# Decay arguments in a Mamba mixer: from six-row matmuls to biased Relus on ScalarE, with the order of three queues changed

## The reference, cut to what matters

```
proj = hidden_states @ in_proj_w.T          # gate (z), x, B, C, dt
hBC  = silu(conv1d(x, B, C; 4 taps))        # B, C shared by 16 of 128 heads
dt   = softplus(dt + dt_bias);  A_dt = -exp(A_log) * dt
A_cumsum = cumsum(A_dt, inside each chunk of 128 tokens)
Lmat = exp(A_cumsum[l] - A_cumsum[s])  for l >= s, else 0
Y_diag = ((C_l . B_s) * Lmat) @ (x * dt)
states = (B * exp(A_cumsum[-1] - A_cumsum))^T @ (x * dt)      # each chunk
new_states: each chunk's state * exp(its last A_cumsum) + the next one's
Y_off  = (C @ carried state) * exp(A_cumsum)
y = rms_norm(Y_diag + Y_off + D * x) * norm_w * silu(gate)
out = y @ out_proj_w.T
```

## Time and profile before

| | |
|---|---|
| profiled execution | 2141.5 us, its span 2139.8 us |
| mean granted clock of TensorE | 0.997 of full |
| TensorE (PE) busy | 2102.7 us, 98% of the span |
| VectorE (DVE) busy | 1689.4 us, 79% |
| ScalarE (ACT) busy | 1401.8 us, 66% |
| GpSimd (POOL) busy | 881.4 us, 41% |
| DMA | 241.89 MB, mean 113 GB/s |
| table loads at the lines of silu and Exp (L1263, L1286) | 127 each, 1283 ns |
| argument matmuls (L1051) | 1024 |

### The profile page before, as it was taken

One profiled execution on the slowest core, in us unless ns is written; L12 is line 12 of the kernel. 1 busy time (PEld: TensorE's weight loads), 2 busy tenths in 40 slices (PEclk: granted clock), 3 DMA queues, 4 the chain that ended last, 5 costly groups with the idle time before them and its releaser, 6 DMA issues.

```text
span 2139.8 us, 37480 instructions
## 1 busy us (share of the span) xinstructions
PE 2102.7 (98%) x13386; PEld 1732.0 (81%) x13386; DVE 1689.4 (79%) x2679; ACT 1401.8 (66%) x1918; POOL 881.4 (41%) x622
## 2 busy tenths in 40 slices
PE   7999998999999999999999999999999999999999
PEld 6788876888888888888888888888888888878887
DVE  7555468988888888888898889898888888876554
ACT  5322277878787777777787877787777778752221
POOL 1222134545454545444454544544544545422221
PEclk9999998999999999999999999999999999999999
DMA  5543224233333333232333333342333233255441
GB/s 201 177 146 138 61 94 125 90 109 103 100 112 101 105 96 108 95 122 91 100 112 101 101 98 114 105 122 96 100 101 112 90 104 109 97 186 177 135 147 40
DMA packets 128644, 241.89 MB, mean 113 GB/s; under 512 B 14048, under 2 KB 48608, under 8 KB 128224
## 3 DMA queue, kind: packets, MB, share of 16 engines
q1 hardware_dynamic: 128480, 239.73, 34.9%
HBM read 234.17 MB, written 5.51 MB: 112 GB/s over the span
## 4 chain that ended last, share of the span: by engine, by line
PE 90%; DVE 3%; issue 3%; ACT 2%; DMA 1%; POOL 1%; SPq 0%; DVEq 0%; POOLq 0%; ACTq 0%
PE ring L1013 35%; PE ring L1113 16%; PE bank L412 6%; PE bank_e L412 6%; PE yt L1094 6%; PE st L1078 4%; PE yt L1100 4%; PE xt L1065 3%; PE bank_e L424 3%; PE bank L424 3%; PE arg L1051 2%; PE xt L1026 1%; PE bank L654 1%; DMA w_raw<-w_in 0%; DVE xr L304 0%
## 5 line engine op out<-in xcount | busy, mean ns | idle before, releaser
L1013 PE MATMUL ring<-m_lnt,w_sb 128*128 128x512 f32 x3456 | 859.9, 399 | 1.2 <-DVE xc L1440 1.2
L1013 PEld LDWEIGHTS ring<-m_lnt,w_sb 128*128 128x128 f32 x3456 | 633.0, 189 | 127.1 <-DVE xc L1440 1.5
L1673 POOL TENSOR_TENSOR w_sb<-w_raw,w_sb 128x512 fp32r<-128x512 f32 x288 | 401.7, 1400 | 177.3 <-ACT w_sb L1246 177.0
L1688 POOL TENSOR_TENSOR ysq<-ysq,y 128x512 f32<-128x512 f32 x126 | 162.8, 1292 | 652.8 <-ACT y L1290 652.8
L1113 PE MATMUL ring<-wo,ygs 128*128 128x512 f32 x1536 | 369.4, 390 | 2.0 <-issue 2.0
L1113 PEld LDWEIGHTS ring<-wo,ygs 128*128 128x128 f32 x1536 | 287.3, 188 | 63.2 <-issue 2.6
L1440 DVE SCALAR_TENSOR_TENSOR xc<-ring,cw,xc 128x511 f32<-128x511 f32 (+2 forms) x384 | 286.0, 745 | 23.0 <-ACT xc L1258 13.9
L1258 ACT ACTIVATE xc<-ring,cb,cw 128x512 f32<-128x512 f32 x128 | 99.2, 775 | 215.4 <-PE ring L1013 215.4
L1678 POOL TENSOR_TENSOR wo<-wo_raw,wo 128x512 fp32r<-128x512 f32 x128 | 214.0, 1672 | 0.0
L1246 ACT ACTIVATE w_sb<-w_raw 128x512 fp32r<-128x512 f32 x288 | 177.0, 619 | 26.8 <-DMA w_raw<-w_in 26.8
L1094 PE MATMUL yt<-em,x_dt 128*64 128x128 f32 x2048 | 183.7, 279 | 3.2 <-DVE state L1482 3.2
(11 more groups left out here) (203 smaller groups left out, 3159.2 us busy)
## 6 DMA issues: line engine op xcount, KB each, us to landing
w_raw<-w_in SPq DMA_DIRECT2D x288, 256.0 KB, 4.2
ce<-e_t SPq DMA_DIRECT2D x128, 384.0 KB, 4.1
wo_raw<-w_out SPq DMA_DIRECT2D x128, 256.0 KB, 4.4
f_gu_q<-gu_w SPq DMA_DIRECT2D x28, 512.0 KB, 3.7
f_gu_zr<-gu_z SPq DMA_DIRECT2D x28, 512.0 KB, 4.5
f_gu_sr<-gu_s SPq DMA_DIRECT2D x28, 512.0 KB, 5.3
f_dn_q<-dn_w SPq DMA_DIRECT2D x28, 256.0 KB, 3.5
f_dn_zr<-dn_z SPq DMA_DIRECT2D x28, 256.0 KB, 4.0
```

The source lines that it names most:

```text
L1013: mm = nc.tensor.matmul(dst[:], w_sb[:, u % WR, wp, k * P:(k + 1) * P], lnt[:, xp, k, b * S:(b + 1) * S], start=(i == 0), stop=(i == 3 * K ...
L1673: nc.gpsimd.tensor_tensor(w_sb[:, u % WR, 1], w_raw[:, u % NR], w_sb[:, u % WR, 0].bitcast(F32), ALU.subtract).then_inc(w_lo, 1)
```

## The change

- `arguments(k)`, the bf16 parts, `a_left`, `a_right` and what fills them go. The float32 sums go to memory (`c_t`), and SP broadcasts the two heads' rows to all partitions, into one of two buffers `cum_b`, two pairs ahead. The sums by token, `cum_q`, come out of one more matmul.
- `clamp(k)`: eight Relus over 128 columns on ScalarE, from and to `cum_b`, with scale -1 and the token's sum as bias. `exponent(k)` is then one Exp from `cum_b` into ARG.
- ScalarE: `clamp(k+1)` stands where `exponent(k)` stood. In odd steps `exponent(k+1)` follows it; in even steps it is the last thing of the step, behind the silus, `y_high`, `square`, and `activate_bc`.
- VectorE: `mask_em(k)` goes ahead of `scale_x(k)` and `gate(k-1)`.
- SP: in each step the next units' weights, then `load_out`, then the sums, then `ce`; `load_gu(0, 0)` of the last step comes behind them.
- The opening of the mixer: Exps of sums of later steps (`later`, `sum_later`) give the decay of the states in place of differences, products and transposes; `sum_chunks` gives each chunk's last Exp; `dt_q` is copied earlier.
- `ysq` has half the size, with `square_sums(0)` five steps earlier.

```diff
+                def clamp(k):
+                    act.wait_ge(c_loaded[k % 2], 16 * (k // 2 + 1))
+                    if k == 0:
+                        act.wait_ge(cumq_done, B)
+                    for h in range(2):
+                        for c in range(CPB):
+                            at = slice(c * CS, (c + 1) * CS)
+                            last = nc.scalar.activation(cum_b[:, k % 2, h, at], cum_b[:, k % 2, h, at], ACT.Relu, scale=-1.0,
+                                                        bias=cum_q[:, k, c, h:h + 1])
+                    last.then_inc(arg_clamped, 1)
+
                 def exponent(k):
-                    act.wait_ge(arg_mm, k + 1)
-                    part = ARG[:].rearrange("p h t -> p (h t)")
-                    nc.scalar.activation(part, part, ACT.Relu, scale=-1.0).then_inc(arg_clamped, 1)
                     act.wait_ge(arg_clamped, k + 1)
-                    nc.scalar.activation(part, part, ACT.Exp, scale=-1.0).then_inc(exp_done, 1)
+                    need(act, em_done, k)
+                    if k == 0:
+                        act.wait_ge(btok_done, 1)
+                        act.wait_ge(decq_done, B)
+                    nc.scalar.activation(ARG[:], cum_b[:, k % 2], ACT.Exp, scale=-1.0).then_inc(exp_done, 1)
...
-                    if k < K:
-                        exponent(k)
+                    if k + 1 < K:
+                        clamp(k + 1)
                     for g in gram_in(k):
                         copy_btok(g)
                     if k + 1 < K:
+                        if k % 2:
+                            exponent(k + 1)
                         activate_x(k + 1)
                         activate_z(k + 1)
...
                         tap(unit)
                         if unit[0] == "c":
                             activate_bc(unit[1])
+                    if k + 1 < K and k % 2 == 0:
+                        exponent(k + 1)
...
-                    if k < K:
-                        scale_x(k)
                     if k == 0:
                         conv(("x", 1))
+                        scale_x(0)
                         decay_c(0)
+                        mask_em(0)
+                    elif k < K:
+                        mask_em(k)
+                        scale_x(k)
                     if 1 <= k <= K:
                         gate(k - 1)
                     if k < K:
-                        mask_em(k)
...
                 for k in range(K):
                     if k > 0:
-                        load_units(k + 1)
-                    if k + 1 < K:
-                        load_args(k + 1)
-                    if k == K - 1:
-
-                        sp.wait_ge(prj_mm, NU)
-                        sp.wait_ge(conv_done, len(CONVED))
-                        tiles.load_gu(sp, 0, 0)
+                        load_units(units_of(k + 1))
                     if 1 <= k < K:
                         load_out(k - 1 if k < K - 1 else K - 1)
                     if k == K - 2:
                         load_out(K - 2)
+                    if k + 2 < K:
+                        load_args(k + 2)
+                    if k + 1 < K:
+                        load_decay(k + 1)
+                    if k == K - 1:
+
+                        sp.wait_ge(prj_mm, NU)
+                        sp.wait_ge(conv_done, len(CONVED))
+                        tiles.load_gu(sp, 0, 0)
```

More of the change, by code:

```diff
@@ L740, in build @@
         a_dt = sbp("a_dt", [P, B, CPB * H])
-        cum = sbp("cum", [P, T, CS])
-        diff = sbp("diff", [P, T, CS])
-        dec_h = sbp("dec_h", [P, B * S])
+        cum = sbp("cum", [P, B * S])
         e_cum = sbp("e_cum", [P, B * S])
-        rest = sbp("rest", [P, B * S])
-        parts = sbp("parts", [P, 3, B * S], BF16)
-        e_end = sbp("e_end", [P, T])
+        later = sbp("later", [P, P])
+        gap_p = sbp("gap_p", [P, 14 * P + 8])
         a_neg = sbp("a_neg", [P, H])
@@ L1339, in scalar @@
                 nc.scalar.activation(low[:], low[:], ACT.Ln, bias=1.0).then_inc(softplus, 1)
+                for b in range(B):
+                    act.wait_ge(adt_done, b + 1)
+                    nc.scalar.activation(dt_q[:, b * JP:(b + 1) * JP],
+                                         (XT, ST)[b][:].rearrange("p (c j h) -> p j c h", c=CPB, h=2), ACT.Copy)\
+                        .then_inc(dtq_done, 1)
                 w_high(("x", 1))
@@ L1342, in scalar @@
                 tap(("x", 0))
+                for b in range(B):
+                    act.wait_ge(cum_mm, b + 1)
+                    nc.scalar.activation(cum[:, b * S:(b + 1) * S], ARG[:, b], ACT.Copy).then_inc(cum_done, 1)
                 w_high(("z", 1))
@@ L1357, in scalar @@
-                activate_x(0)
-                nc.scalar.activation(e_end[:], cum[:, :, CS - 1], ACT.Exp).then_inc(cum_exp, 1)
-                act.wait_ge(rest_done, 2)
-                nc.scalar.activation(parts[:, 1], rest[:], ACT.Copy).then_inc(parts_done, 1)
-                act.wait_ge(rest_done, 1)
-                nc.scalar.activation(diff[:], diff[:], ACT.Exp).then_inc(cum_exp, 1)
-                act.wait_ge(rest_done, 3)
-                nc.scalar.activation(parts[:, 2], rest[:], ACT.Copy).then_inc(parts_done, 1)
@@ L1366, in scalar @@
+                for b in range(B):
+                    act.wait_ge(dec_mm, b + 1)
+                    part = (YT, ARG[:, 0])[b][:, 0:OFFC * H]
+                    nc.scalar.activation(part, part, ACT.Exp).then_inc(dec_exp, 1)
+                act.wait_ge(last_mm, 1)
+                nc.scalar.activation(e_last[:].rearrange("p b c h -> p (b c h)"), ARG[:, 1], ACT.Exp).then_inc(last_done, 1)
+                w_high(("x", 2))
                 tap(("x", 1))
                 copy_btok(0)
-                act.wait_ge(last_mm, 1)
@@ L1369, in scalar @@
-                nc.scalar.activation(e_last[:].rearrange("p b c h -> p (b c h)"), ST[:], ACT.Copy).then_inc(last_done, 1)
+                clamp(0)
+                exponent(0)
                 def factor_root(b):
@@ L1536, in vector @@
                     norm_low(dve, nm, t)
+                nc.vector.tensor_scalar(later[:], tri[:], -1.0, 1.0, ALU.mult, ALU.add).then_inc(later_done, 1)
                 conv(("b", 0))
@@ L1681, in sum_squares @@
                 def sum_squares(k):
-                    part = ysq[:, batch(k) * S:(batch(k) + 1) * S]
+                    part = ysq[:]
+                    if k == JP:
+                        pool.wait_ge(ssq_mm, 1)
                     pool.wait_ge(y2_done, k + 1)
```

202 lines of the change are left out of this document (82 added, 120 removed).

## The result

The changed kernel takes 2169.83 us (median of 4 runs, 2167.52 to 2171.91) against 2141.31 (4 runs, 2140.67 to 2141.75): ratio 1.0133, 95% interval 1.0116 to 1.0151. The forecast was slower, 2157 us in 2126 to 2175. The sign is right and the time lies in the range, near its upper end; the size is +28.5 us where +15.6 was said. The profiled execution took 2171.91 us, its span is 2170.2, and TensorE's mean clock 0.991 of full.

The account below looks back on a forecast made before the run. TensorE's list was taken to bound the even part of the mixer. From 2141.5 us the terms -42.2 + 36.8 + 12 + 8 + 1 = +15.6 gave 2157 us, range 2126 to 2175.

Parts of the forecast that it names:

- TensorE's saving: TensorE's chain in each pair: dropping the eight argument matmuls saves 0.33 us, 42.2 us over 128 pairs.
- late pair: Pair bringing in the C tile: late Exp and earlier mask stall gram 2.45 us, 15 times, +36.8 us.
- clock after it: After the 15 pauses before gram: TensorE's clock falls in half, 1.6 us each, +12 us, from 0 to +24.
- end of the mixer: Mixer's end: load_gu behind load_out makes sub_gu, last states and outputs late, +8 us, between +1 and +12.
- opening: Mixer's opening: replaced operations, earlier weights and late taps of steps 1 to 5, +1 us, from -5 to +5.
- ScalarE in an ordinary pair: Ordinary pairs: eight Relus take 2.4 us, net +0.1 us within 2.5 us of rest, nothing on the path.
- rival 3: ScalarE becomes the bound: eight Relus at 3.2 us, up to 12 us more in late-tap pairs, 2169 us; chance 0.1.
- rival 1: Late pair: gram finds its bank free and the saving shows, 2108 us; chance 0.2 together with the half-stalled case.
- the forecast's chain: Late pair: tap, convolution, mask and x_dt run late, so gram waits for its bank about 2.4 us.
- Rival 2: Late pair: the stall is there but the clock holds, 2143 us, no measurable change; chance 0.17.
- the forecast's own 2146 to 2172: Whole kernel: range of the forecast alone, with clock term 0 to 24, end and opening varied.
- Rival 1 with half the stall: Late pair: half the gram stall and no clock falls, 2126 us; chance 0.2 together with the no-stall case.

Follow-up runs that it names:

- run 3: Changed kernel with VectorE's mask put back behind the scalings and gate, where it stood before: 2225.75 us, ratio 1.0393.
- run 5: Changed kernel with the Exp ahead of the silus of x and z only in the fifteen even steps with a C tile: 2156.07 us, ratio 1.0065.
- run 6: Changed kernel with the Exp ahead of the silus in every step, giving back all 128 table loads for Exp: 2227.58 us, ratio 1.0401.
- run 11: run 9 plus the edits of run 7 and run 1, with step 0's Exp ahead of the silus and B's tap right behind the clamps: 2132.91 us.
- run 9: Changed kernel with C's tap and the Exp right behind z's silu in C steps, silu of B and C last: 2128.81 us, ratio 0.9941.
- run 4: Changed kernel with the output weight copies for the pair after the C tile done a step earlier, ahead of C's tap: 2171.51 us, ratio 1.0134.
- run 1: Changed kernel with load_gu(0, 0) ahead of load_out again on SP in the last step: 2162.42 us, ratio 1.0091.
- run 7: Changed kernel with the next layer's first subtraction, sub_gu(0, 0), moved behind the last carry on VectorE: 2160.25 us, ratio 1.0083.

## Why the forecast was right, and where its size came from

The terms come first. Each pair has one row of `turn_x` in either trace; a pair's excess is the distance of two starts after, less that before, plus 0.31. The late pairs are those of step 5 of each group; of their 48.6 us of excess, the 6.8 by which the five that fell exceed the others are the clock's. The end is what the spans differ by beyond the last `turn_x` (1898.18 after, 1879.37 before), again with 0.31 added.

| term | forecast | measured |
|---|---|---|
| TensorE's saving, 128 pairs | -42.2 | -39.7 (0.31 each) |
| late pair, 15 times | +36.8 | +41.8 (2.79 each, falls taken out) |
| clock after it | +12 | +6.8 (5 falls) |
| end of the mixer | +8 | +11.9 |
| opening | +1 | +3.0 |
| single pairs, numbers 66 to 98 | 0 | +6.6 |
| sum | +15.6 | +30.4 |

*TensorE's saving.* Right; no cost of changing the tiling showed. The chain has 0.33 for the argument group, but what it gave back is 0.31 in every ordinary pair.

*ScalarE in an ordinary pair.* Right: 2.44 us for the eight, table loads 65 and 66 at the two lines, no pair of this kind waits. The Trainium skill's figure for a table switch (ScalarE: Activation LUTs, "What ACT_TABLE_LOAD costs", about 2.7 us) would have made the late Exp, by an estimate from that figure, 1.4 us later than the rows do. The trace after disagrees with it as the one before did: the Exp starts 1.30 us after the load does (481.53, 482.83). What the forecast didn't see is how near ScalarE's list is to its limit: rival 3 was priced by the list's length, with the rest of 2.5 us as cover. Runs 3, 5, 6 and 11 show that this rest is not free. It is bounded by the mask, or by the landing of the next weights, on one side and by z's silu, which frees a bank, on the other, and 0.66 us in the wrong place costs 1 us a group. In the change as made rival 3 didn't come; without the halved loads (run 6) or the earlier mask (run 3) ScalarE is late by more than that rival had. The forecast's 64 loads at each line were off by one and two.

*The late pair.* The mechanism was right in cause (the load and the Exp ahead of the next tap), in place and in count, and 2.45 us was close to the 2.3 that the named wait shows; run 9 took it away and gave 41 us back. Two things were off. First, the operation that waits: the forecast said of the two weight copies behind the Exp that they were not late. `wo_high` was, and `project_out` waits for it; `gram` is 0.15 us behind. By the forecast's own sign (about fifteen waits of 2.4 us at `gram`; none there, then rival 1) the trace alone spoke against it. Run 4 shows that the forecast's chain was there and that the time is the same by either. That the overlooked chain was as long as the forecast one, and not longer, was luck. Second, even without a named wait this pair keeps 0.4 us more than its saving allows (12.85 in run 9 against 12.76 - 0.31), 6 us over the groups. The starts of the matmuls in group 3's pair place it, against before: `project_out` begins 0.22 us later behind the projection of z, `gram` 0.13 later behind `project_out`, and the states 0.09 later behind `gram`. The forecast had no term for it, and no run here explains it.

*The clock.* Five falls of fifteen, where half were said, and 1.4 us each, where 1.6 was. The pauses are alike, 2.14 to 2.27 us, in those that fell and those that didn't. Rival 2 (no fall at all) was off by 6.8 us in this term, the forecast by 5.2.

*The end.* The step was right (SP's order, `sub_gu`, mask, states), the sum was too small: `load_gu` went out at 1898.80, right behind `load_out`. Against the last `turn_x` that is 8.7 us later than before, where 7.2 was said. Its third transfer took 7.3 us to land and not 5.3 (it was asked for at 1899.69, and `sub_gu` could start at 1906.96). The 1 MB for the last norm was asked for right behind it, a load that the forecast did not have; that it slowed the transfer is not shown. Runs 1 and 7 each take one link away: with the order on SP mended 7.4 us come back, with the order on VectorE 9.6, and with both 12. These don't add up, since either link alone breaks most of the chain.

*The opening.* Forecast +1 in -5 to +5, measured +3.0: within the bound, but the late taps of the first steps did come, as 5.2 and 3.6 us of wait at states, and the earlier weights gave nothing visible against them.

*The range.* The terms at their ends together, with the clock at 0 or 24, the end at 1 or 12 and the opening at -5 or +5, give 2132 to 2177, wider than the forecast's own 2146 to 2172. The 2126 to 2175 that counts was set wider than that own range, but stops 2 us under the upper end. Rival 1 with half the stall adds up to 2127, not 2126.

*Single pairs.* This step was left out. In the middle of the mixer z's silu is late by 1.3 us for the ring, twice (the wait for sz L1259 in the list above). At the first of the two ScalarE has computed a root for the norm (L1379) behind the late Exp. The root needs its own table load, and so the Exp of the odd step, which elsewhere finds its table in place, has a load ahead of it, and the silus behind it. Timeline of ScalarE and TensorE:

```profile
1146.70 1.28 ACT L1379 ACT_TABLE_LOAD   x1
...
1153.48 1.28 ACT L1289 ACT_TABLE_LOAD   x1
...
1158.28 3.02 PE L1011 MATMUL ring<-m_lnt,w_sb 128*128 128x512 f32 x12 [1.27 <-ACT sz L1259]
```

The second, at 1361.95, has no root ahead of it (the next is at 1364.14). There, in a step with a B tile, the weight copy ahead of the clamps waits 1.78 us for its transfer, and what made that late was not followed. The rest of the 6.6 comes in the pairs around the two, and was not taken apart.

So between the two spans +30.4 stands in place of +15.6 (+28.5 by the medians). That is five small losses and one gain against the forecast: 2.5 + 5.0 - 5.2 + 3.9 + 2.0 + 6.6 = 14.8 us between the two sums. The direction stood on one term, the late pair, and that one was forecast to within 5 us.

## What to carry to other kernels

An instruction moved to the end of an in-order engine's list must be followed through everything that stands behind it, the humble copies too: the wait that shows first may hide another of the same length, and a run that takes only the named one away gives nothing. Where an engine rests, ask what bounds the rest on both sides before using it as cover; the same load and Exp cost 41 us at one place of ScalarE's list, 27 to 28 at two others, and bring no wait that the views name in the hole between z's silu and C's convolution, against which the others are counted. A change that reads as one idea was four here: the argument off TensorE gained about 40 us, the odd and even order and the early mask paid for the clamps, and one position and one queue order gave all of it away.

## What was not expected of the hardware

- After fifteen pauses of TensorE of 2.14 to 2.27 us the clock fell five times, and then twelve matmuls took 4.57 us, not 3.00. The length of the pause doesn't tell the ones from the others. The place does in part: none of the seven in groups 2 to 8 fell, in after nor in the profiled executions of runs 1, 4 and 7, which have pauses as long in the same pairs; of the seven in groups 9 to 15 three to five fell, and not the same ones in all four. Why is open. It also differs between executions of one kernel: in run 1 one of four ran at a mean clock of 0.997 and took 2156.64 us, the others at 0.991 to 0.993 and 2161.66 to 2163.67.
- The table load before the Exp started only when the wait for the mask had ended (475.28 in run 5, behind 1.26 us of idle), while the load before the silu of B and C ran ahead of its wait (473.93 in run 9, with 1.46 us of idle behind it). A load may or may not hide in its own instruction's wait; whether another order of the two waits of the Exp would hide it was not tried.
- Eight Relus in place over 128 columns with a bias pointer take 2.44 us, 0.305 each, as the rows of before had let one estimate.
